# Writing out the expert loops of a two-layer gated transformer, with index columns read in place and deeper slots for rows and results

## What is computed

```python
# layer 0: 8 experts, hidden width 1024, the best 2 of 8 for each token
h1 = gelu(einsum('bth,efh->btef', x, w1) + b1)
expert_outputs = einsum('btef,ehf->bteh', h1, w2) + b2
mixed = sum(take(expert_outputs, topk_indices) * topk_weights)
# layer 1: 15 experts, hidden width 512, the best 3 of 15, and one shared expert of width 1024
# shared_enc: the shared expert; router_enc: sum over the chosen experts of gate * (gelu(x_norm @ rW1 + rb1) @ rW2 + rb2)
x = x + tanh(g_ffn[1]) * (shared_enc + router_enc + x_norm)
```

## Time and profile before

| what | us |
|---|---|
| runs (3): median, lowest, highest | 1464.58, 1462.56, 1466.8 |
| the profiled execution: its own time | 1459.17 |
| the profiled execution: span from first to last instruction | 1457.4 |
| busy in the span: PE, DVE, ACT, POOL | 1204.5, 629.4, 488.4, 390.6 |
| first expert loop, first to last tile's transpose | 376.42 to 594.17 |
| second expert loop, first to last tile's transpose | 1193.48 to 1405.00 |
| mean granted TensorE clock, share of full speed | 0.929 |

### The profile page before, as it was taken

One profiled execution on the slowest core, in us unless ns is written; L12 is line 12 of the kernel. 1 busy time (PEld: TensorE's weight loads), 2 busy tenths in 40 slices (PEclk: granted clock), 3 DMA queues, 4 the chain that ended last, 5 costly groups with the idle time before them and its releaser, 6 DMA issues. The chain is left out here.

```text
span 1457.4 us, 31104 instructions
## 1 busy us (share of the span) xinstructions
PE 1204.5 (83%) x11472; PEld 928.7 (64%) x11472; DVE 629.4 (43%) x1495; ACT 488.4 (34%) x1117; POOL 390.6 (27%) x419
## 2 busy tenths in 40 slices
PE   4888888844799999717999999998759999998870
PEld 3666666534699999704566656665546678887760
DVE  4666666537211111056555556565343702222215
ACT  2444444411133333213444444444332312222221
POOL 2544454420222222121000000000026124444432
PEclk9999999975799999959999999999859999999995
DMA  4010111013799999471000000000050229999965
GB/s 129 15 27 27 31 37 28 7 46 112 275 325 321 329 328 333 145 223 43 22 14 28 25 18 25 18 17 5 13 153 0 73 87 309 315 325 303 318 209 172
DMA packets 74575, 190.60 MB, mean 131 GB/s; under 512 B 10536, under 2 KB 46824, under 8 KB 66024
## 3 DMA queue, kind: packets, MB, share of 16 engines
q1 hardware_dynamic: 66264, 165.16, 34.5%
q0 software_dynamic: 8064, 22.03, 4.3%
q10 hardware_dynamic: 144, 1.97, 0.4%
HBM read 168.29 MB, written 20.84 MB: 130 GB/s over the span
## 5 line engine op out<-in xcount | busy, mean ns | idle before, releaser
L1586 ACT ACTIVATE ex_hT<-ex_h,ex_w 128x128 f32<-128x128 f32 x464 | 132.6, 368 | 337.3 <-PE ex_h L1655 195.1
L1655 PE MATMUL ex_h<-ex_xT,ex_w 128*128 128x128 f32 x1856 | 224.3, 277 | 0.0
L1655 PEld LDWEIGHTS ex_h<-ex_xT,ex_w 128*128 128x128 f32 x1856 | 216.3, 194 | 0.6
L1664 PE MATMUL ex_y<-ex_w,ex_hT 128*128 128x256 f32 x928 | 213.9, 379 | 0.0
L1664 PEld LDWEIGHTS ex_y<-ex_w,ex_hT 128*128 128x128 f32 x928 | 170.1, 190 | 19.7
L1333 POOL DMA_INDIRECT ex_results<-ex_yt,ex_to x84 | 82.9, 987 | 275.9 <-DVE ex_yt L1541 169.3
L272 DVE TENSOR_REDUCE at_negmax<-at_scores 120x8 bf16<-120x800 f32 (+1 forms) x96 | 90.6, 985 | 86.8 <-PE at_scores L459 86.8
L865 ACT ACTIVATE at_probs<-at_scores 120x800 f32<-120x800 f32 (+2 forms) x128 | 100.6, 842 | 72.9 <-PE at_scores L977 72.9
L212 POOL TENSOR_TENSOR at_sum<-at_probs 120x800 f32<-120x800 f32 (+1 forms) x48 | 78.4, 1633 | 141.1 <-ACT at_probs L383 141.1
L705 DVE TENSOR_REDUCE at_negmax<-at_scores 100x2 f32<-100x722 f32 x128 | 115.1, 899 | 0.0
L383 ACT ACTIVATE at_probs<-at_scores 120x800 f32<-120x800 f32 (+1 forms) x96 | 80.1, 835 | 103.3 <-PE at_scores L468 103.1
(11 more groups left out here) (240 smaller groups left out, 1848.3 us busy)
## 6 DMA issues: line engine op xcount, KB each, us to landing
ex_w<-in_pack_in SPq DMA_DIRECT2D x32, 1028.0 KB
ex_w<-in_pack_out SPq DMA_DIRECT2D x32, 1024.0 KB
ex_w<-in_pack_in SPq DMA_DIRECT2D x52, 514.0 KB
ex_w<-in_pack_out SPq DMA_DIRECT2D x52, 512.0 KB
at_ctx<-in_ctxT SPq DMA_DIRECT2D x32, 361.0 KB, 3.3
x<-at_x SPq DMA_DIRECT2D x32, 100.0 KB
ex_x<-x SPq DMA_DIRECT2D x8, 400.0 KB
ex_normed<-ex_xhat SPq DMA_DIRECT2D x8, 400.0 KB
```

The costliest lines, as they stand in the source:

```text
L1586: last = act.activation(hT[s][:, c, :], ps_h[:, bank, i * P:(i + 1) * P], ACT.Gelu, bias=w1[s][:, B1 + c:B1 + c + 1])
L1655: last = pe.matmul(ps_h[:, bank, i * P:(i + 1) * P], w1[s][:, c * ff + f:c * ff + f + P], xT[s][:, c, :], start=(c == 0), stop=(c == KC - 1))
L1664: last = pe.matmul(ps_y[:, s, 0:D], hT[s][:, c, :], w2[s][:, c * D:(c + 1) * D], start=(c == 0), stop=(c == FC - 1))
```

## The change

`rounds` and its hardware loops are gone: all tiles are written out on every engine, with Python integers for tile numbers, so every wait is for a constant and the `turns` increments go. The copies `index_from` and `index_to` are gone: the indirect DMAs read column t of from_row and to_row, behind one new wait on POOL for `rows_ready`. Gathered rows get 6 slots and results 4, in place of 3 and 3. The wait for b2_loaded is made once, ahead of DVE's loop. The orders of SP, PE and ACT are as before.

```diff
-        N = 3
+        N, GATHERS, SCATTERS = 3, 6, 4
-        gi, si = slots("from", [P, 1], U32), slots("to", [P, 1], U32)
+        xt = [m.sb(f"xt{i}", [P, D]) for i in range(GATHERS)]
+        yt = [m.sb(f"yt{i}", [P, D]) for i in range(SCATTERS)]
...
             @block.gpsimd
+                def gather(t):
+                    need(pool, xT_ready, t - GATHERS + 1)
+                    pool.indirect_dma_start(xt[t % GATHERS][:, :], None, xhd,
+                                            bass.IndirectOffsetOnAxis(from_row[:, t:t + 1], 0)).then_inc(gathered[t % GATHERS], 16)
+
+                def scatter(t):
+                    pool.wait_ge(y_taken, t + 1)
+                    pool.indirect_dma_start(ways, bass.IndirectOffsetOnAxis(to_row[:, t:t + 1], 0),
+                                            yt[t % SCATTERS][:, :], None).then_inc(scattered[t % SCATTERS], 16)
...
                 pool.wait_ge(xhat_saved, 16 * NG)
-                rounds(pool, step, 3, 1, NT)
+                pool.wait_ge(rows_ready, 1)
+                for t in range(-GATHERS, NT + 1):
+                    if live(t + GATHERS):
+                        gather(t + GATHERS)
+                    if live(t - 1):
+                        scatter(t - 1)
...
             @block.vector
+                    dve.sem_inc(rows_ready, 1)
-                def index_from(t, s, rnd):
-                    need(dve, gathered[s], rnd * 16)
-                    dve.sem_inc(dve_turns, 1)
-                    dve.tensor_copy(gi[s][:, :], from_row[:, col(t)]).then_inc(from_ready, 1)
-
-                def index_to(t, s, rnd):
-                    need(dve, scattered[s], rnd * 16)
-                    dve.sem_inc(dve_turns, 1)
-                    dve.tensor_copy(si[s][:, :], to_row[:, col(t)]).then_inc(to_ready, 1)
...
-                    dve.wait_ge(b2_loaded, 16)
-                    e = dve.value_load(expert_of[0:1, col(t)], min_val=0, max_val=E - 1)
+                    e = dve.value_load(expert_of[0:1, t:t + 1], min_val=0, max_val=E - 1)
                     dve.wait_ge(y_ready, t + 1)
-                    need(dve, scattered[s], rnd * 16)
-                    dve.sem_inc(dve_turns, 1)
+                    need(dve, scattered[t % SCATTERS], t // SCATTERS * 16)
...
                 dve.wait_ge(expert_ready, 1)
-                rounds(dve, step, 3, 1, NT)
+                dve.wait_ge(b2_loaded, 16)
+                for t in range(-1, NT + 1):
+                    if live(t + 1):
+                        take_xT(t + 1)
+                    if live(t - 1):
+                        take_y(t - 1)
```

More of the change, by code:

```diff
@@ L1099, in __call__ @@
         self.eng.wait_ge(self.sem, self.n)
[L1102 to L1115, removed]
 def experts(nc, consts, name, x_in, x_out, router, router_b, pack1, pack2, b2, top, ff, shared):
@@ L1243, in shared_bank @@
             return (ps_h[0:T, 2, 0:D], ps_t[0:T, 1, 0:D])[n % 2]
-        def col(t):
-            return slice(t, t + 1) if isinstance(t, int) else bass.ds(t, 1)
         def live(t):
-            return not isinstance(t, int) or 0 <= t < NT
+            return 0 <= t < NT
         with nc.Block() as block:
@@ L1300, in _ @@
                 sp.wait_ge(expert_ready, 1)
-                rounds(sp, step, 3, 1, NT)
-                for s in range(N):
-                    sp.wait_ge(scattered[s], 16 * len(range(s, NT, N)))
+                for t in range(-3, NT):
+                    if live(t + 3):
+                        load_in(t + 3)
+                    if live(t + 2):
+                        load_out(t + 2)
+                for s in range(SCATTERS):
+                    sp.wait_ge(scattered[s], 16 * len(range(s, NT, SCATTERS)))
                 if shared:
@@ L1575, in _, with hidden_gelu @@
             def _(act):
[L1576 to L1586, removed]
-                                                      bias=w1[s][:, B1 + c:B1 + c + 1])
-                            last.then_inc(h_taken, 1)
+                def hidden_gelu(t):
+                    for u in range(U):
+                        act.wait_ge(h_ready, t * U + u + 1)
+                        if u == 0:
+                            need(act, y_ready, t - N + 1)
+                        for i in range(UNIT):
+                            c = u * UNIT + i
+                            last = act.activation(hT[t % N][:, c, :], ps_h[:, (t * U + u) % N, i * P:(i + 1) * P], ACT.Gelu,
+                                                  bias=w1[t % N][:, B1 + c:B1 + c + 1])
+                        last.then_inc(h_taken, 1)
                 for i in range(B // 2):
@@ L1628, in _ @@
                     act.dma_start(b2all, b2.partition_broadcast(P)).then_inc(b2_loaded, 16)
-                rounds(act, step, 0, 1, NT)
+                for t in range(NT):
+                    hidden_gelu(t)
                 for i in range(NG * top):
@@ L1638, in _, with turn, hidden @@
             def _(pe):
-                def turn(t, s, rnd):
-                    pe.wait_ge(gathered[s], (rnd + 1) * 16)
+                def turn(t):
+                    pe.wait_ge(gathered[t % GATHERS], (t // GATHERS + 1) * 16)
                     need(pe, xT_taken, t)
                     for c in range(KC):
-                        last = pe.transpose(ps_t[:, 0, c * P:(c + 1) * P], xt[s][:, c * P:(c + 1) * P], ident[:, :])
+                        last = pe.transpose(ps_t[:, 0, c * P:(c + 1) * P], xt[t % GATHERS][:, c * P:(c + 1) * P], ident[:, :])
                     last.then_inc(xT_ready, 1)
-                def hidden(t, s, rnd):
-                    pe.wait_ge(w1_in[s], (rnd + 1) * 16)
+                def hidden(t):
+                    pe.wait_ge(w1_in[t % N], (t // N + 1) * 16)
                     pe.wait_ge(xT_taken, t + 1)
@@ L1743, in _ @@
                     shared_result(3)
-                rounds(pe, step, 1, 1, NT)
+                for t in range(-1, NT + 1):
+                    if live(t + 1):
+                        turn(t + 1)
+                    if live(t):
+                        hidden(t)
+                    if live(t - 1):
+                        result(t - 1)
 def build(nc, a, out):
```

66 lines of the change are left out of this document (20 added, 46 removed).

## The result

| | us |
|---|---|
| kernel before, median of 4 runs (lowest, highest) | 1463.57 (1462.14, 1466.8) |
| changed kernel, median of 4 runs (lowest, highest) | 1446.28 (1445.24, 1449.4) |
| ratio, 95% interval | 0.9889, 0.9859 to 0.9919 |
| profiled execution: before, changed | 1459.17, 1446.95 |
| its span: before, changed | 1457.4, 1445.2 |

The two profiled executions differ by 12.2 us in span only: the second loop's first transpose came 4.8 us later in the new one. What other stages took longer in this one execution isn't put down to the change.

The account below looks back on a forecast made before the run. It took PE to bound the first loop and late gathers to hold PE up in the second. Terms -0.4 - 15.2 + 7.8 - 0.3 + 0.3 gave -7.8 us, from 1464.58 to 1456.8 us; 8-in-10 range 1448 to 1467.

Parts of the forecast that it names:

- the period of the second loop: Second loop, tiles 3 to 51: early gathers cut the period from 4.216 to 3.90 us, -15.2 us in all.
- the rival with 12%: Second loop: DMA packets overlap better than the share tells, PE becomes the bound at 3.76 us a tile, 1450.1 us; 12%.
- First loop, 0: First loop's inside: PE's own work, 7.24 us a tile, is the bound and isn't touched, so no gain.
- First loop's start, -0.4 us: First gather goes out sooner behind the last index table without three copies between; -0.4 us, bounds 0 and -1.2.
- Gathers issued early end the waits at L1643: Second loop: gathers issued six tiles ahead end PE's waits at the transposes of gathered rows, 25.7 + 13.5 us.
- The bias wait, +7.8 us: Second loop's start: DVE's first xT copy waits for the bias table, PE stands still, clock falls; +7.8 us, bounds +5.8 and +9.6.
- Ends, -0.3 us: Behind the last turn, both stages: fewer DVE and POOL waits and no paired increments; -0.3 us, bounds 0 and -1.
- Fetching, +0.3 us: Both loops: fetching the longer written-out code takes DMA time, some 20 packets a loop; +0.3 us, bounds 0 and +2.
- The signs that the prediction named: Second loop: no wait at L1643, few waits for weights, DMA share 0.97 or more, tiles 3 to 51 in 187 us.
- DMA is the bound already: Second loop: late gathers only show full DMA queues; share ends at 0.95, period 4.127 us, 1467.7 us; 15%.
- the gathers aren't what PE waits for: Second loop: another part of DVE's or POOL's turn ends the waits, so the period stays, 1472.0 us; 5%.

Follow-up runs that it names:

- e6: Changed kernel plus a load of 256 KB more, which nothing reads, for each tile of the second loop; period 3.915 us, 1454.19 us (1 run).
- e5: Changed kernel plus a load of 512 KB more, which nothing reads, for each tile of the second loop; period 4.508 us, 1481.54 us (1 run).
- e4: Changed kernel with three slots for gathered rows and three for results; 1456.78 us, 0.9979 of the kernel before.
- e8: Changed kernel with three slots for gathered rows and four for results; 1451.89 us, 0.993 of the kernel before.
- e7: Changed kernel with six slots for gathered rows and three for results; 1442.19 us, 0.9877 of the kernel before.
- e11: Kernel of e1 with four slots for gathered rows and three for results; 1436.86 us, 0.9831 of the kernel before.
- e3: Kernel before with only its hardware loops written out; copies, three slots and paired increments kept; 1461.06 us, ratio 1.0006.
- e9: Changed kernel with the index copies on DVE kept, each for its slot; 1445.88 us, 0.9896 of the kernel before.
- e1: Changed kernel with the wait for the bias table back at the first take_y; 1436.52 us, 0.9842 of the kernel before.
- e10: Changed kernel with 32 unread identity matmuls on PE between the second loop's first and second transposes; 1444.68 us, 0.9878 of the kernel before.

## Why the prediction was wrong

**The step that failed is the period of the second loop, "At a share of 0.98 to 1.00 the DMA period is 3.92 to 4.00 us ... I take 3.90".** It took the DMA share as linear in bytes, so that 4.216 us at 0.93 would be 3.92 us at 1. Measured: at 0.93 311 GB/s, at 0.97 348, at 1.02 to 1.03 about 405. The period came out at 3.755 us, PE's own time, and the term is -22.1 us instead of -15.2. The row that contradicted it stood in the prediction's own list, 394 GB/s at 1.00, and was put aside for the larger share of small rows in this loop; in e6 and e5, with small rows in the mixture, though a smaller part of it, the ceiling is no lower. What the prediction held for the rival with 12%, PE as the bound at 3.76 us, is what happened; its time, 1450.1, is still 3.8 us over the measured median, since that rival carried the other terms of the forecast.

By its other steps:

- *First loop, 0*: right. 7.248 us a tile before and after, and in every experiment.
- *First loop's start, -0.4 us*: right in kind, and nearly in size. The first gather goes out 0.94 us behind the last table instead of 1.25, and 0.94 or 0.95 in every kernel without the copies, 1.22 to 1.26 in those with them: 0.3 us. The first transpose came 0.4 us sooner in this pair, but that distance varies by 0.3 us among kernels whose code there is the same.
- *Gathers issued early end the waits at L1643*: right in kind, and shown: e4 and e8 (with three slots for rows the waits stay), e7 (with six they are gone, whatever the result slots), e11 (four are enough). The prediction named two reasons for late gathers, the short lead and DVE's wait for an old scatter ahead of the next copy. The second is worth 0.23 us a tile at most while the lead is three tiles (e3 against e4), and with six slots nothing that the runs can show (e9).
- *The bias wait, +7.8 us*: 7.15 us against the old start, and 9.5 us against the same kernel without it (e1), since the old start had some 2.3 us of late gather in it. Its parts came out at 7.1 us of standing and 2.4 us of clock (e10), where the forecast had 7.8 and 2.3 us.
- *Ends, -0.3 us*: from tile 51's transpose to the end 52.4 us before, 50.4 after. That stretch varies from 50.1 to 54.4 us over the experiments, whose code there is the same but for the scatters' waits and increments, so these 2.0 us aren't put down to the change. What is, is 0.6 us of them: a scatter now leaves that much sooner behind take_y (the rows stand at the end of this document).
- *Fetching, +0.3 us*: 11 packets of 16 KB in 1211 to 1400 instead of the 20 reckoned for a loop, and no sign of it in either period. e3, written out and nothing else, has the ratio 1.0006.

With the terms that the runs show the sum is -0.3 - 22.1 + 7.15 - 0.6 = -15.85 us. The median moved by 17.3, and the interval of the ratio allows 12 to 21 us, so the 1.4 us between them can't be told from noise. The period alone, put right in the forecast, would have given 1449.9 us, inside its range; that the measured median lies under the range owes some 1 us to the bias wait and the fetching, which cost less than forecast, and the rest to what the runs can't assign.

The signs that the prediction named would not have told it from its rival: no wait at the transposes, few waits for weights and a share of 0.97 all came as written. Only the time from tile 3 to tile 51 told the two apart: 180.24 us, where 187 was forecast.

The rivals "DMA is the bound already" and "the gathers aren't what PE waits for" fell with e6, where the DMA engines moved 402 GB/s, and with e7. The second had the Trainium skill's fit behind it ("DMA: Bandwidth & Descriptors", section "Anatomy of one DMA — SWDGE (gpsimd) path"). The trace agrees with that fit where next to nothing else is under way: the last scatter of the changed kernel, 128 KB, lands 2.41 us behind its issue, as this row of its chain of waits says (start us, us, what), and the fit gives an estimated 2.3 us.

```profile
1404.81 2.41 DMA ex_results<-ex_yt,ex_to_row
```

In the loaded loop the gathers' median was 5.7 us, and the fit can't be used for a lead there (DMA issues in 1211 to 1400: what, queue, times, median us to landing):

```profile
ex_xt<-ex_normed,ex_from_row POOLq DMA_INDIRECT x44, 5.7
```

## What to carry to other kernels

When an engine waits a little at one kind of input and never at the others, give that input one slot more first, and measure it alone: here four slots did what six did (e11), and written-out loops (e3), columns read in place (e9) and more result slots (e7, e8) gave nothing that can be told from noise. (No run has more slots in the old loop alone.) Follow a wait that is moved ahead of a loop to everything behind it on its engine; here a wait that was only made earlier cost 9.5 us, against the 22.1 us that the period gained. And don't extrapolate a busy share to a ceiling: load the resource until something waits for it, and read the bytes.

## What the runs showed of the hardware

- The share of the DMA engines isn't a measure of what is left: 311 GB/s at 0.93 and 348 at 0.97 in the same loop with the same pieces, 401 to 410 at 1.02 to 1.03 with a load more for each tile (e6, e5).
- On POOL, the two paired increments ahead of a scatter cost 0.6 us. Timeline of the last take_y and scatter in the kernel before, in the changed kernel, and in e9; from the end of the one to the start of the other it is 0.89 us (1414.83 to 1415.72), 0.28 us (1404.53 to 1404.81) and 0.28 us. e9 still waits for the index copy and has no increments; e3, written out with the increments kept, has 0.89 us again. So it is neither the second wait nor the registers:

```profile
1414.41 0.42 DVE L1541 TENSOR_TENSOR ex_yt<-ex_y,ex_sw 128x256 f32<-128x256 f32 x1 [1.30 <-PE ex_y L1664]
1415.72 0.97 POOL L1333 DMA_INDIRECT ex_results<-ex_yt,ex_to  x1 [0.76 <-issue]
```

```profile
1404.11 0.42 DVE L1500 TENSOR_TENSOR ex_yt<-ex_y,ex_sw 128x256 f32<-128x256 f32 x1 [1.30 <-PE ex_y L1615]
1404.81 0.97 POOL L1303 DMA_INDIRECT ex_results<-ex_yt,ex_to_row  x1 [0.75 <-DVE ex_yt L1500]
```

```profile
1403.28 0.42 DVE L1513 TENSOR_TENSOR ex_yt<-ex_y,ex_sw 128x256 f32<-128x256 f32 x1 [1.30 <-PE ex_y L1634]
1403.98 0.97 POOL L1308 DMA_INDIRECT ex_results<-ex_yt,ex_to  x1 [0.76 <-DVE ex_yt L1513]
```

- Behind a wait of 7.7 us in which PE did nothing the granted clock was 0.50 (1.2 GHz), which cost 1.7 to 2.5 us; matmuls on an identity matrix, whose result nothing reads, kept it at 1.00 through the same wait (e10).
